# Parameter chains divided over VectorE and GpSimd, and both rotation products of a state-space block on GpSimd

## The chip, the cores and the metric

One core of a Trainium2 chip runs the whole program. The metric is device time in microseconds (us). Each time below is of one execution or is said to be a median.

## What is computed

The input `x` has the shape (16, 96, 16, 16): 16 batches, 96 channels, 256 tokens each. The output is `x + block(group_norm(x))`:

```python
fx = layernorm(tokens(group_norm(x)), ln1_g, ln1_b)          # groups of 3 channels, then over 96 channels
step = exp(log_step); lam_bar = exp(lam * step)               # 48 complex modes
mask = (step * abs(lam_im) / (2 pi) < 0.25)
B_bar = ((lam_bar - 1) / lam)[:, None] * Bc
x_t = lam_bar * x_(t-1) + B_bar fx_t                           # scan over the 256 tokens
y = 2 * real((Cc * mask) x_t) + D * fx
fy = layernorm(gelu(y) + fx, ln2_g, ln2_b)
z1, z2 = split(fy @ W_enc.T)
out = x + (z1 * gelu(z2)) @ W_dec.T + fy
```

## The kernel before

**Tiling.** The batches are two halves of eight, called H = 0 and H = 1. A half is 96 partitions by 2048 columns, in 4 tiles of 512. TensorE has four PSUM banks for each half. The scan takes the 256 tokens as 32 blocks of T = 8 tokens: inside a block VectorE runs seven steps (`scan`), across blocks four doublings follow (`doubled`, `doubling`).

**First stage of a half.** VectorE takes `bn_stats` of each batch (`statistics`). `group_norm(H)` makes mean, variance and 1/sigma of the groups, with two small matmuls on TensorE (`group_mean`, `group_variance`) and a Newton iteration on VectorE (`inverse_root`), in which each instruction waits for the one before it. `scale_centering(H, n)` then writes the matrix `pm` of batch n (96x96), and `center_batch(H, n)` multiplies the batch by it on TensorE. ScalarE evacuates the result twice (`squares`, `centered_values`). TensorE sums the squares (`variances`), VectorE makes 1/sigma of every token (`inverse_sigma`, twelve dependent instructions on 128x128), TensorE spreads it (`broadcast`), and VectorE multiplies (`scale_tile`, to `fx`). The matmuls of `inputs` multiply `fx` by the matrix `um`.

**The parameters.** `um` comes from a chain on 96x1 and 96x13 numbers. In `parameters()` VectorE makes exp(log_step), the angles (`ANG`, reduced to `RED`), the decays (`EXM`, `RK`); ScalarE makes two sines of `RED`; VectorE makes `COS` and `NSS` and the matrix `bst`. GpSimd makes `rotT` = identity times `COS` in one 96x768 product (L267), and VectorE adds swap times `NSS` in eight instructions (L789, recorded at L664). TensorE multiplies `bst` by `rotT` (L593, L594), and ScalarE evacuates `um` (L398, L400). `output_tables()` makes what the outputs need. When it has ended (`tables_ready`, L819), GpSimd makes the matrices `rotX` (three 96x576 instructions) and then `yl` (three 96x768 instructions, and a fourth for `yl[:, 1]`), L303 to L308.

**What sets the order.** The parameter chains are generators, and each of their steps is put by hand between instructions of the normalisation on VectorE (`parameter_steps`, L951 to L975): six steps first, one behind each `bn_stats`, one behind each instruction of `group_norm`, one after every second `scale_centering`, and the rest in `inverse_sigma(0, 0)`. All engines run their instructions in the order written. TensorE's order around the change (L561 to L611): warm-up matmuls, `group_mean(0)`, `group_variance(0)`, `center_batch(0, 0..5)`, `group_mean(1)` (which waits for the last `bn_stats` of the second half), `center_batch(0, 6..7)`, `group_variance(1)`, `variances(0, 0, ..)`, all eight `center_batch(1, n)`, two `variances` of the second half, the product for `um` (waits `bst_ready`, `rot_ready`), `broadcast(0, 0)`, `inputs(0, i)` with the other two `variances`, three small matmuls to `vecs`, then `direct` and `local_outputs` of three tiles (wait `yl_ready`), `seed_sum(0)` (waits `rotx_ready`) and `broadcast(0, 1)` (waits for `inverse_sigma(0, 1)`). Every TensorE instruction is recorded at line L424; an fp32 matmul shows as two records.

Of the kernel before, what the change touches and what calls it, by code (L numbers as in the profile page):

```python
# [34 lines left out]
ALU = mybir.AluOpType  # L35
# [7 lines left out]
T = 8  # L43
NA = L // T
HB = B // 2
# [10 lines left out]
WARM = (10, 2, 14)  # L56
WARM_N = 256
FIRST_PM = 4
GROUP = 3
NGRP = GROUP * L  # L60
GN_EPS = 1e-5
# [27 lines left out]
def s5_block(nc, x, small, mats, mask_in, out):  # L89
    ctx = ExitStack()  # L90
    with ctx:
# [22 lines left out]
        rotT = sb("rotT", [96, T, 96])  # L114
# [29 lines left out]
        par_steps = sem("par_steps")  # L144
# [5 lines left out]
        cos_ready = sem("cos_ready")  # L150
        rotcos_ready = sem("rotcos_ready")
# [4 lines left out]
        tables_ready = sem("tables_ready")  # L156
        rotx_ready = sem("rotx_ready")
        yl_ready = sem("yl_ready")
        dm_ready = sem("dm_ready")
        bcm_ready = sem("bcm_ready")  # L160
# [92 lines left out]
        def _(pool):  # L253
# [6 lines left out]
            def settle():  # L260
# [5 lines left out]
            pool.wait_ge(cos_ready, 1)  # L266
            nc.gpsimd.tensor_tensor(  # L267
                rotT[:, :, :], m(M_ID).unsqueeze(1).broadcast_to([96, T, 96]),
                tbl(COS, T).unsqueeze(2).broadcast_to([96, T, 96]), ALU.mult).then_inc(rotcos_ready, 1)
            pool.wait_ge(in_mats, 16)  # L270
# [45 lines left out]
        def _(act):  # L316
# [10 lines left out]
            nc.scalar.activation(tbl(SH), tbl(RED), ACT.Sin, scale=0.5).then_inc(sines_ready, 1)  # L327

# [46 lines left out]
            def gelu_y(H):  # L375

                for i in range(NT):
# [9 lines left out]

            group_bias(0)
# [7 lines left out]
            squares(1, 2, 6)  # L396
# [5 lines left out]
            squares(1, 6, HB)  # L402
# [19 lines left out]
        def _(pe):  # L422
# [26 lines left out]
            def center_batch(H, n):  # L449

                pe.wait_ge(pm_ready, HB * H + n + 1)
                mm(bank(H, n // 2)[0:96, L * (n % 2):L * (n % 2 + 1)], pm[:, HB * H + n, :],
                   xs[:, HB * H + n, :]).then_inc(centered[0], 1)
# [18 lines left out]
            def broadcast(k, H):  # L472

                pe.wait_ge(inv_ready[k], H + 1)
                for i in range(NT):
                    if k == 0:
                        pe.wait_ge(taken[0], HB * H + 2 * (i + 1))
                        if H == 0 and i >= 2:
                            pe.wait_ge(um_ready, i - 1)
# [110 lines left out]
            pe.wait_ge(taken[0], HB)  # L590
            pe.wait_ge(bst_ready, 1)
            pe.wait_ge(rot_ready, T)
            mm(bank(0, 2)[0:97, 0:480], bst[:, :], rotT[:, 0:5, :])  # L593
            mm(bank(0, 3)[0:97, 0:288], bst[:, :], rotT[:, 5:8, :]).then_inc(umat_done, 1)  # L594
            pe.wait_ge(bcm_ready, 1)
            broadcast(0, 0)
# [65 lines left out]
        def _(dve):  # L662
# [33 lines left out]
            norm, par = Steps(norm_steps), Steps(par_steps)  # L696

            def expm1(p, y, arg):

                par.next_ts(y, arg, 1 / 128, -80 / 128, ALU.mult, ALU.max)  # L700
                yield
                par.next_ts(p, y, 1 / 120, None, ALU.mult)
                yield
                for c in (1 / 24, 1 / 6, 1 / 2, 1.0):
                    par.next_stt(p, p, c, y, ALU.add, ALU.mult)
                    yield
                for _ in range(7):
                    par.next_stt(p, p, 2.0, p, ALU.add, ALU.mult)
                    yield

            def parameters():


                par.next_stt(scol(REC), s(LS), -1.0, s(LS), ALU.mult, ALU.max)
                yield
                yield from expm1(scol(EXP), scol(Y1), scol(REC))
                par.next_ts(scol(EXP1), scol(EXP), 1.0, None, ALU.add)
                par.add(scaled(scol(NEG), s(LS), 0.0, None, ALU.is_lt))
                par.add(scaled(scol(POS), s(LS), 0.0, None, ALU.is_ge))
                yield  # L720
                par.settle()
                par.add(nc.vector.reciprocal(scol(REC1), scol(EXP1)))
                yield
                par.next_tt(scol(T4), scol(REC1), scol(NEG), ALU.mult)
                yield
                par.next_stt(scol(STEP), scol(EXP1), scol(POS), scol(T4), ALU.mult, ALU.add)
                yield
                par.next_tt(scol(TH), s(LI), scol(STEP), ALU.mult)
                par.add(nc.vector.tensor_tensor(scol(RE), s(LR), scol(STEP), ALU.mult))
                yield  # L730
                par.next_ts(tbl(ANG), s(KV, NK), scol(TH), None, ALU.mult)
                par.add(scaled(tbl(XK), s(KV, NK), scol(RE), None, ALU.mult))
                yield

                par.next_ts(tbl(NRND), tbl(ANG), 1 / (2 * np.pi), ROUND, ALU.mult, ALU.add)
                yield
                par.next_ts(tbl(NRND), tbl(NRND), -ROUND, None, ALU.add)
                yield
                for part in (TWO_PI_HI, TWO_PI_MID, TWO_PI_LO):
                    par.next_stt(tbl(ANG), tbl(NRND), -float(part), tbl(ANG), ALU.mult, ALU.add)  # L740
                    yield
                par.settle()
                scaled(tbl(RED), tbl(ANG), PI_BELOW, -PI_BELOW, ALU.min, ALU.max).then_inc(angles_ready, 1)
                yield
                yield from expm1(tbl(EXM), tbl(TMP), tbl(XK))

                dve.wait_ge(sines_ready, 2)
                par.next_tt(tbl(SH2), tbl(SH), tbl(SH), ALU.mult)
                par.add(scaled(tbl(NSS), tbl(SIN), s(RHO), None, ALU.mult))
                par.add(scaled(tbl(RK), tbl(EXM), 1.0, None, ALU.add))  # L750
                yield
                par.next_ts(tbl(CM1), tbl(SH2), -2.0, None, ALU.mult)
                par.add(nc.vector.tensor_tensor(tbl(RSIN), tbl(RK), tbl(SIN), ALU.mult))
                par.add(nc.vector.tensor_tensor(scol(T2), s(LR), s(LR), ALU.mult))
                yield
                par.settle()
                scaled(tbl(COS), tbl(CM1), 1.0, None, ALU.add).then_inc(cos_ready, 1)
                par.add(nc.vector.tensor_tensor(scol(T3), tbl(RSIN, 1, 1), s(LI), ALU.mult))
                par.add(stt(scol(DEN), s(LI), s(LI), scol(T2), ALU.mult, ALU.add))
                yield  # L760

                dve.wait_ge(cos_ready, 1)
                par.next_tt(scol(T1), tbl(EXM, 1, 1), tbl(COS, 1, 1), ALU.mult)
                par.add(nc.vector.reciprocal(scol(DEN), scol(DEN)))
                yield
                par.next_tt(scol(T1), scol(T1), tbl(CM1, 1, 1), ALU.add)
                yield
                par.next_tt(scol(T4), scol(T1), s(LI), ALU.mult)
                par.add(stt(scol(CRE), scol(T1), s(LR), scol(T3), ALU.mult, ALU.add))
                yield  # L770
                par.next_stt(scol(CIM), tbl(RSIN, 1, 1), s(LR), scol(T4), ALU.mult, ALU.subtract)
                par.add(nc.vector.tensor_tensor(scol(CRE), scol(CRE), scol(DEN), ALU.mult))
                yield
                par.next_stt(scol(CIM), scol(CIM), scol(DEN), s(RHO), ALU.mult, ALU.mult)
                yield
                dve.wait_ge(in_mats, 16)
                par.next_ts(bt1[:, :], m(M_BS), scol(CIM), None, ALU.mult)
                yield
                par.next_stt(bst[:, 0:C], m(M_B), scol(CRE), bt1[:, :], ALU.mult, ALU.add)
                yield  # L780
                par.next_tt(bt1[:, :], bst[:, 0:C], m(M_B1), ALU.mult)
                yield
                par.settle()
                nc.vector.reduce_sum(bst[:, C:C + 1], bt1[:, :], axis=mybir.AxisListType.X).then_inc(bst_ready, 1)
                yield

                dve.wait_ge(rotcos_ready, 1)
                for b in range(T):
# [37 lines left out]
            def parameter_steps(count):  # L826

                for _ in range(count):
                    next(input_steps, None)
# [258 lines left out]
```

## Time and profile before

| what | us |
|---|---|
| median of 3 runs | 116.42 |
| the 3 runs | 110.52, 117.62, 116.42 |
| the profiled execution | 110.42 |
| its span, first to last instruction | 108.6 |
| TensorE, VectorE, ScalarE, GpSimd busy | 94.9, 77.6, 41.0, 31.9 |
| mean granted TensorE clock | 0.961 |

The profiled execution is 1.8 us longer than its span, and agrees with the shortest of the three runs. Times in the rows are counted from the start of the span. Engines are PE (TensorE), PEld (its weight loads), DVE (VectorE), ACT (ScalarE), POOL (GpSimd), SP (SyncE); a queue has a q behind its name.

### The profile page before, as it was taken

The numbers are of one execution on the slowest core, as the hardware profiler recorded it, in microseconds if no ns is written. First come the engines' busy times: TensorE is split into PE (matmuls) and PEld (weight loads), VectorE is DVE, ScalarE is ACT, GpSimd is POOL, SyncE is SP. The second block draws the span as 40 slices with busy tenths as digits, with TensorE's granted clock in tenths as the row PEclk, the third lists the DMA queues.
The fourth block names the chain that finished last, engine by engine and source line by source line (L and its number), as shares of the span: only waits on it lengthen the run. The fifth ranks groups of instructions, "written<-read, shape, count | busy, mean of one in ns | idle before, by whom it ended". The sixth has DMA issues, their size and how long they took to land.

```text
span 108.6 us, 1488 instructions
## 1 busy us (share of the span) xinstructions
PE 94.9 (87%) x502; PEld 56.2 (52%) x502; DVE 77.6 (71%) x260; ACT 41.0 (38%) x79; POOL 31.9 (29%) x26
## 2 busy tenths in 40 slices
PE   5999897269989929999899999999599999999960
PEld 4668766146555715676476655567324432533310
DVE  1688999999986899658677302389990289994590
ACT  2254167807449100024037009818049722024200
POOL 8600000400049992000018000007995000296000
PEclk9999999955799999999999999999999999999997
DMA  2997000000000000000000000000000000450135
GB/s 77 275 262 168 3 0 0 6 0 0 0 0 0 0 0 3 0 6 0 0 0 0 0 0 3 6 0 0 0 0 0 0 0 0 118 149 29 28 84 177
DMA packets 3767, 3.79 MB, mean 35 GB/s; under 512 B 496, under 2 KB 3664, under 8 KB 3760
## 3 DMA queue, kind: packets, MB, share of 16 engines
q1 hardware_dynamic: 3392, 3.49, 12.3%
q10 hardware_dynamic: 368, 0.20, 0.8%
q8 instruction: 4, 0.07, 0.3%
q14 instruction: 3, 0.02, 0.1%
HBM read 2.12 MB, written 1.57 MB: 34 GB/s over the span
## 4 chain that ended last, share of the span: by engine, by line
PE 70%; DVE 21%; issue 4%; ACT 1%; DVEq 1%
PE ps L424 70%; DVE st L836 2%; DVE fy L664 2%; DVE pm L885 2%; DVE sc L694 2%; DVE rs L664 1%; DVE upper L668 1%; DVE sq L664 1%; DVE tb L664 1%; DVE tb L668 1%; DVE y L982 1%; DVE gn L664 1%; DVE rs L694 1%; DVE fx L664 1%; DVE sc L664 1%
## 5 line engine op out<-in xcount | busy, mean ns | idle before, releaser
L424 PE MATMUL ps<-fy,mt 96*96 96x512 f32 x32 | 14.9, 600 | 1.3 <-DVE fy L664 1.3
L290 POOL TENSOR_TENSOR y<-gl,fx 96x512 f32<-96x512 f32 x4 | 6.1, 1524 | 29.8 <-ACT gl L379 29.8
L298 POOL TENSOR_TENSOR res<-fy,xs 96x512 f32<-96x512 f32 x8 | 10.7, 1359 | 11.6 <-DVE fy L664 11.5
L424 PE MATMUL ps<-xs,pm 96*96 96x256 f32 x32 | 10.8, 492 | 3.3 <-DVE pm L885 3.3
L385 ACT ACTIVATE y<-ps,vecs 96x512 f32<-96x512 f32 x8 | 5.5, 687 | 16.4 <-PE ps L424 16.4
L664 DVE SCALAR_TENSOR_TENSOR w<-ps,vecs,y 96x512 f32<-96x512 f32 x8 | 5.9, 743 | 7.4 <-ACT y L385 7.4
L424 PE MATMUL ps<-fx,dm 96*96 96x512 f32 x16 | 8.4, 605 | 2.6 <-issue 2.2
L933 DVE TENSOR_TENSOR Z<-Z,ps 96x240 f32<-96x240 f32 (+3 forms) x8 | 2.8, 355 | 9.5 <-PE ps L424 9.5
L424 PEld LDWEIGHTS ps<-fy,mt 96*96 96x96 f32 x32 | 5.0, 163 | 8.7 <-issue 6.8
L424 PEld LDWEIGHTS ps<-xs,pm 96*96 96x96 f32 x32 | 6.4, 214 | 5.9 <-DVE pm L885 3.8
L379 ACT ACTIVATE gl<-ps,db 96x512 f32<-96x512 f32 x8 | 5.5, 684 | 9.4 <-PE ps L424 9.4
L424 PE MATMUL ps<-wm 96*96 96x256 f32 x20 | 7.9, 586 | 1.2 <-DVE wm L949 1.2
L424 PE MATMUL ps<-fx,um 97*96 97x256 f32 x32 | 8.2, 390 | 0.2 <-DVE fx L664 0.2
L424 PE MATMUL ps<-w,yl 96*96 96x256 f32 x32 | 8.2, 379 | 0.0
L664 DVE SCALAR_TENSOR_TENSOR w<-w,tb,ps 96x256 f32<-96x256 f32 x14 | 6.6, 471 | 1.9 <-ACT w L366 1.2
L424 PE MATMUL ps<-w,mt 96*96 96x512 f32 x16 | 7.8, 602 | 0.0
L424 PEld LDWEIGHTS ps<-w,yl 96*96 96x96 f32 x32 | 5.2, 163 | 5.1 <-issue 4.0
L358 ACT ACTIVATE sq<-ps,vecs 96x512 f32<-96x512 f32 x8 | 5.5, 686 | 6.2 <-PE ps L424 6.2
L424 PE MATMUL ps<-y,mt 96*96 96x512 f32 x16 | 7.7, 595 | 0.1
L340 ACT ACTIVATE sq<-ps,gn 96x256 f32<-96x256 f32 x16 | 6.5, 470 | 2.7 <-PE ps L424 2.6
L424 PE MATMUL ps<-Z,yl 96*96 96x256 f32 x32 | 7.2, 379 | 0.0
L424 PEld LDWEIGHTS ps<-wm 96*96 96x96 f32 x20 | 5.1, 262 | 3.6 <-DVE wm L949 1.2
(112 smaller groups left out, 168.1 us busy)
## 6 DMA issues: line engine op xcount, KB each, us to landing
out_dram<-sq SPq DMA_DIRECT2D x8, 192.0 KB, 2.2
xs<-x_dram SPq DMA_DIRECT2D x3, 384.0 KB, 6.1
xs<-x_dram SPq DMA_DIRECT2D x2, 192.0 KB, 3.5
mt<-mats_dram SPq DMA_DIRECT2D x1, 338.6 KB, 6.8
mt<-mats_dram ACTq DMA_DIRECT2D x1, 180.0 KB, 3.9
sm<-small_dram ACTq DMA_DIRECT2D x1, 8.6 KB, 2.8
cmask<-mask_dram ACTq DMA_DIRECT2D x1, 9.0 KB, 4.9
```

What stands on the lines that cost most here:

```text
L290: nc.gpsimd.tensor_tensor(yv[:, RT * i:RT * (i + 1), :], cols(gl, H, i).rearrange("c (b m) -> c b m", b=RT), cols(fx, H, i).rearrange("c ( ...
L298: nc.gpsimd.tensor_tensor(cols(res, H, i), cols(fy, H, i), xs[:, HB * H + 2 * i:HB * H + 2 * i + 2, :].rearrange("c n l -> c (n l)"), ALU. ...
L340: nc.scalar.activation(t[:, H, :].rearrange("c (b n a) -> c n b a", b=T, n=HB)[:, n], bank(H, n // 2)[0:96, L * (n % 2):L * (n % 2 + 1)].r ...
L358: nc.scalar.activation(cols(sq, H, i), bank(H, i)[0:96, :], ACT.Square, bias=vecs[:, 2:3]).then_inc(squared[1], 1)
L379: nc.scalar.activation(cols(gl, H, i), bank(H, i)[0:96, :], ACT.Gelu, bias=db[:, 0:1]).then_inc(gl_ready, 1)
L385: nc.scalar.activation(cols(gz, H, i), bank(*Z2[H, i])[0:96, :], ACT.Gelu, bias=vecs[:, 1:2]).then_inc(gz_ready, 1)
L424: return nc.tensor.matmul(o, lhsT, rhs, start=start, stop=stop)
L664: return nc.vector.scalar_tensor_tensor(out=o, in0=a, scalar=sca, in1=b, op0=op0, op1=op1)
L668: return nc.vector.tensor_scalar(o, a, s1, None, op0)
L694: self.add(nc.vector.tensor_tensor(*a))
L836: nc.vector.bn_stats(st[:, HB * H + q, :], xs[:, HB * H + q, :]).then_inc(gn_stats, 1)
L933: nc.vector.tensor_tensor(zd, zd, o[:, :, d:], ALU.add).then_inc(z_ready, 1)
```

## The change

The work of `parameters()` and `output_tables()` is divided.

- VectorE keeps one generator `step_chain()`: step size, angle unit `TH` (`angle_unit_ready`), decays (`decay_ready`), and the chain to `bst`. It is taken two steps behind each of the first eight `bn_stats`, then one at a time.
- GpSimd makes the angles (ten dependent 96x13 instructions), `COS` and `NSS` (`cos_ready`), `rotS` = swap times `NSS` and `rotC` = identity times `COS` (two 96x768 products), the output tables, `db` and `dm`; after `inv_ready[0]` it makes `yl` first and `rotX` second. The eight VectorE instructions on `rotT` are gone.
- ScalarE makes `pm` of batches 2 to 7 of the first half (FIRST_PM = 2).
- TensorE adds 14 warm-up matmuls ahead of `center_batch(1, 0)`, does four `center_batch(1, n)`, then the product for `um` from `rotS` and `rotC` with twice the matmuls, then `broadcast(0, 0)` with `center_batch(1, 4)` and `(1, 5)` inside, then the last two and two `variances`.

```diff
-WARM = (10, 2, 14)
+WARM = (10, 2, 14, 14)
-FIRST_PM = 4
+FIRST_PM = 2
...
# GpSimd
-            pool.wait_ge(cos_ready, 1)
+            pool.wait_ge(angle_unit_ready, 1)
+            ts(tbl(ANG), s(KV, NK), scol(TH), None, ALU.mult)
+            settle()
+            ts(tbl(NRND), tbl(ANG), 1 / (2 * np.pi), ROUND, ALU.mult, ALU.add)
+            settle()
+            ts(tbl(NRND), tbl(NRND), -ROUND, None, ALU.add)
+            for part in (TWO_PI_HI, TWO_PI_MID, TWO_PI_LO):
+                settle()
+                ts(tbl(RED), tbl(NRND), -float(part), None, ALU.mult)
+                settle()
+                tt(tbl(ANG), tbl(RED), tbl(ANG), ALU.add)
+            settle()
+            nc.gpsimd.tensor_scalar(tbl(RED), tbl(ANG), PI_BELOW, -PI_BELOW, ALU.min,
+                                    ALU.max).then_inc(angles_ready, 1)
...
+            pool.wait_ge(sines_ready, 2)
+            tt(tbl(SH2), tbl(SH), tbl(SH), ALU.mult)
+            settle()
+            ts(tbl(CM1), tbl(SH2), -2.0, None, ALU.mult)
+            settle()
+            nc.gpsimd.tensor_scalar(tbl(COS), tbl(CM1), 1.0, None, ALU.add).then_inc(cos_ready, 1)
+            nc.gpsimd.tensor_scalar(tbl(NSS), tbl(SIN), s(RHO), None, ALU.mult).then_inc(cos_ready, 1)
...
+                rotS[:, :, :], m(M_SW).unsqueeze(1).broadcast_to([96, T, 96]),
+                tbl(NSS, T).unsqueeze(2).broadcast_to([96, T, 96]), ALU.mult).then_inc(rot_ready, 1)
...
+                rotC[:, :, :], m(M_ID).unsqueeze(1).broadcast_to([96, T, 96]),
+                tbl(COS, T).unsqueeze(2).broadcast_to([96, T, 96]), ALU.mult).then_inc(rot_ready, 1)
...
+            pool.wait_ge(inv_ready[0], 1)
...
-            pool.wait_ge(tables_ready, 1)
+            combine(yl, M_C, tbl(CU, T), M_CS, tbl(SU, T), T).then_inc(yl_ready, 1)
             combine(rotX, M_ID, tbl(XCO, NX), M_SW, tbl(XSI, NX), NX).then_inc(rotx_ready, 1)
-            combine(yl, M_C, tbl(CU, T), M_CS, tbl(SU, T), T).then_inc(yl_ready, 1)
# ScalarE, behind the two sines
+            for n in range(FIRST_PM, HB):
+                scale_centering(n)
...
-            squares(1, 2, 6)
+            squares(1, 2, 4)
             act.wait_ge(umat_done, 1)
...
# TensorE
+            warm_up(WARM[3], bank(1, 0))
             center_batch(1, 0)
             group_bias(1)
-            center_batch(1, 1)
-            for i in range(1, NT):
-                if i == NT - 1:
-                    pe.wait_ge(bias_ready, 2)
-                center_batch(1, 2 * i)
-                center_batch(1, 2 * i + 1)
+            for n in range(1, 4):
+                center_batch(1, n)
+            pe.wait_ge(taken[0], HB)
+            pe.wait_ge(bst_ready, 1)
+            pe.wait_ge(rot_ready, 2)
+            for part, first, last in ((2, 0, 5), (3, 5, 8)):
+                o = bank(0, part)[0:97, 0:96 * (last - first)]
+                mm(o, bst[:, :], rotS[:, first:last, :], stop=False)
+                last_mm = mm(o, bst[:, :], rotC[:, first:last, :], start=False)
+            last_mm.then_inc(umat_done, 1)
+            pe.wait_ge(bcm_ready, 1)
+            broadcast(0, 0, lambda: (center_batch(1, 4), center_batch(1, 5)))
+            pe.wait_ge(bias_ready, 2)
+            center_batch(1, 6)
+            center_batch(1, 7)
             variances(0, 1, 0)
             variances(0, 1, 1)
# VectorE
+            step_chain_on(6)
             for q in range(HB):
                 statistics(0, q)
-                parameter_steps(1)
+                step_chain_on(2)
             dve.wait_ge(in_early, 16)
             statistics(1, 0)
+            group_norm(0, lambda j: step_chain_on(1), lambda: (statistics(1, 1), statistics(1, 2)))
+            for n in range(FIRST_PM):
                 scale_centering(0, n)
+            for q in range(3, HB):
                 statistics(1, q)
+                step_chain_on(1)
+            group_norm(1, lambda j: step_chain_on(1), lambda: step_chain_on(2))
+            scale_centering(1, 0)
+            scale_centering(1, 1)
+            inverse_sigma(0, 0, lambda j: scale_centering(1, j + 3) if j < 1 else step_chain_on(1))
+            for n in range(4, HB):
+                scale_centering(1, n)
```

## Rows read from the trace of the kernel before

**Rows 1.** The page's first part: busy us, share of the span, instructions.
```profile
PE 94.9 (87%) x502; PEld 56.2 (52%) x502; DVE 77.6 (71%) x260; ACT 41.0 (38%) x79; POOL 31.9 (29%) x26
```

**Rows 2.** The chain that ended last: start us, us, what.
```profile
22.35 0.27 DVE pm L885
...
22.66 8.81 PE ps L424 x38
...
32.21 5.63 PE ps L424 x46
37.84 2.21 issue
40.05 6.44 PE ps L424 x26
```

**Rows 3.** Windows: stretch, length, busy us of the engines, granted clock, DMA.
```profile
21.50:22.00 0.50, 0.00 (x0) 0.00 (x0) 0.47 (x5) 0.00 (x0) 0.00 (x0) 0.74 0.00 0
...
22.60:28.00 5.40, 5.34 (x14) 3.76 (x15) 5.36 (x29) 2.56 (x7) 0.00 (x0) 0.50 0.00 0
...
28.50:29.00 0.50, 0.50 (x3) 0.33 (x2) 0.50 (x3) 0.50 (x2) 0.00 (x0) 0.93 0.00 0
```

**Rows 4.** Timeline of GpSimd and of VectorE beside it: start us, us, instruction.
```profile
4.30 0.12 POOL L264 MEMSET Z<- 96x16 f32 x1
...
18.85 1.47 POOL L267 TENSOR_TENSOR rotT<-mt,tb 96x768 f32<-96x768 f32 x1 [14.42 <-DVE tb L668]
...
19.07 1.27 DVE L694 TENSOR_TENSOR sc<-tb 96x1 f32<-96x1 f32 x1
...
31.47 1.15 POOL L280 TENSOR_TENSOR rotX<-mt,tb 96x576 f32<-96x576 f32 x1 [11.15 <-DVE db L819]
...
31.72 2.72 DVE L664 SCALAR_TENSOR_TENSOR fx<-xc,sm,ps 96x512 f32<-96x512 f32 x4 [0.22 <-PE ps L424]
...
38.15 1.80 POOL L283 TENSOR_TENSOR yl<-yl 96x768 f32<-96x768 f32 x1
...
38.47 1.63 DVE L664 SCALAR_TENSOR_TENSOR rs<-rs 128x128 f32<-128x128 f32 x1
```

**Rows 5.** Timeline of VectorE in the first stage.
```profile
3.57 0.15 DVE L664 SCALAR_TENSOR_TENSOR sc<-sm 96x1 f32<-96x1 f32 x1 [2.43 <-DMA sm<-small_dram]
3.76 0.15 DVE L669 TENSOR_SCALAR sc<-sc 96x1 f32<-96x1 f32 x1
...
7.83 0.14 DVE L664 SCALAR_TENSOR_TENSOR sc<-sc 96x1 f32<-96x1 f32 x1
7.89 0.41 DVE L836 BATCH_NORM_STATS2 st<-xs 96x6 f32<-96x256 f32 x1
...
9.28 0.17 DVE L864 TENSOR_REDUCE gn<-ps 96x8 f32<-96x16 f32 x1 [0.50 <-PE ps L424]
...
17.48 0.17 DVE L864 TENSOR_REDUCE gn<-ps 96x8 f32<-96x16 f32 x1 [0.15 <-PE ps L424]
```

**Rows 6.** Timeline of TensorE, first and second half's first stage.
```profile
14.20 1.95 PE L424 MATMUL ps<-xs,pm 96*96 96x256 f32 x8
...
18.62 1.10 PE L424 MATMUL ps<-sq,mt 96*32 96x128 f32 x32
22.66 1.17 PE L424 MATMUL ps<-xs,pm 96*96 96x256 f32 x2 [2.94 <-DVE pm L885]
...
29.93 1.53 PE L424 MATMUL ps<-rotT,bst 96*97 96x480 f32 x4
31.29 0.61 PE L424 MATMUL ps<-parts,bcm 128*96 128x128 bf16 x8
...
34.58 2.83 PE L424 MATMUL ps<-fx,um 97*96 97x256 f32 x12
```

**Rows 7.** Groups of VectorE by shape, first 32 us: busy us, mean ns.
```profile
L664 DVE SCALAR_TENSOR_TENSOR rotT<-mt,tb,rotT 96x96 f32<-96x96 f32 x8 | 2.5, 309 | 0.0
```

**Rows 8.** Timeline of VectorE in two calls of inverse_sigma: end of one, a bare one.
```profile
28.76 0.34 DVE L664 SCALAR_TENSOR_TENSOR parts<-upper,cmask,rs 128x128 bf16<-128x128 bf16 x1
...
70.15 0.29 DVE L669 TENSOR_SCALAR rs<-ps 128x128 f32<-128x128 f32 x1 [0.76 <-PE ps L424]
...
75.03 0.35 DVE L664 SCALAR_TENSOR_TENSOR parts<-upper,cmask,rs 128x128 bf16<-128x128 bf16 x1
```

More of the change, by code:

```diff
@@ L113, in s5_block @@
         mt = sb("mt", [96, NM])
-        rotT = sb("rotT", [96, T, 96])
+        rotC = sb("rotC", [96, T, 96])
+        rotS = sb("rotS", [96, T, 96])
         rotX = sb("rotX", [96, 2, NX, 96])
@@ L159, in s5_block @@
         dm_ready = sem("dm_ready")
+        db_ready = sem("db_ready")
+        angle_unit_ready = sem("angle_unit_ready")
+        cos_ready = sem("cos_ready")
+        decay_ready = sem("decay_ready")
+        pm_act = sem("pm_act")
         bcm_ready = sem("bcm_ready")
@@ new lines, in _ @@
+            tt(scol(MR), scol(MASK), s(NRHO), ALU.mult)
+            ts(scol(MI), scol(MASK), -1.0, None, ALU.mult)
+            ts(tbl(SSG), tbl(SIN), s(NRHO), None, ALU.mult)
+            settle()
+            ts(tbl(CU), tbl(COS), scol(MR), None, ALU.mult)
+            ts(tbl(SU), tbl(SIN), scol(MI), None, ALU.mult)
+            pool.wait_ge(decay_ready, 1)
+            for dst, unit in ((XCO, COS), (XSI, SSG)):
+                ts(tbl(dst, 1, 0), tbl(unit, 1, T), tbl(RK, 1, 1), tbl(RK, 1, 0), ALU.mult, ALU.mult)
+                ts(tbl(dst, 1, 1), tbl(unit, 1, K16), tbl(RK, 1, 1), tbl(RK, 1, T), ALU.mult, ALU.mult)
+                tt(tbl(dst, 4, 2), tbl(unit, 4, K16), tbl(RK, 4, K16), ALU.mult)
@@ L375, in gelu_y @@
             def gelu_y(H):
+                act.wait_ge(db_ready, 1)
                 for i in range(NT):
@@ L401, in _ @@
                                  ACT.Copy).then_inc(um_ready, 1)
-            squares(1, 6, HB)
+            squares(1, 4, HB)
             centered_values(1, 2, HB)
@@ L470, in variances, with broadcast @@
                     last.then_inc(variance[k], 1)
-            def broadcast(k, H):
+            def broadcast(k, H, between=None):
                 pe.wait_ge(inv_ready[k], H + 1)
@@ L477, in broadcast @@
                         pe.wait_ge(taken[0], HB * H + 2 * (i + 1))
+                        if H == 0 and i == 2:
+                            between()
                         if H == 0 and i >= 2:
@@ L694, in next_tt @@
                     self.add(nc.vector.tensor_tensor(*a))
[L696 to L788, printed above, removed]
-                    stt(rotT[:, b, :], m(M_SW), tbl(NSS, 1, b), rotT[:, b, :],
-                        ALU.mult, ALU.add).then_inc(rot_ready, 1)
-                    yield
@@ L824, in _ @@
-            input_steps, output_steps = parameters(), output_tables()
-            def parameter_steps(count):
-                for _ in range(count):
-                    next(input_steps, None)
+            norm = Steps(norm_steps)
             def statistics(H, q):
@@ L855, in inverse_root, with group_norm @@
                 norm.next_stt(y, u, 5.0, y, ALU.add, ALU.mult)
-            def group_norm(H, between=lambda: None, after=lambda: None):
+            def group_norm(H, between=lambda j: None, after=lambda: None):
                 var, t, u, minus, scale, shift = [gn[:, H, k, 0:HB] for k in
@@ L949, in _, with step_chain_on @@
+            steps = step_chain()
+            def step_chain_on(count):
+                for _ in range(count):
+                    next(steps, None)
             nc.vector.memset(wm[:, :], 1.0).then_inc(wm_ready, 1)
             dve.wait_ge(in_small, 16)
-            parameter_steps(6)
+            step_chain_on(6)
             for q in range(HB):
                 statistics(0, q)
-                parameter_steps(1)
+                step_chain_on(2)
             dve.wait_ge(in_early, 16)
             statistics(1, 0)
-            group_norm(0, lambda: parameter_steps(1), lambda: (statistics(1, 1), parameter_steps(2)))
@@ L967, in _ @@
-            for n in range(FIRST_PM):
-                scale_centering(1, n)
-                parameter_steps(1)
-            inverse_sigma(0, 0, lambda j: scale_centering(1, FIRST_PM + 1 + j) if j < HB - FIRST_PM - 1
-                          else parameter_steps(1))
-            for _ in input_steps:
-                pass
-            for _ in output_steps:
+                step_chain_on(1)
+            group_norm(1, lambda j: step_chain_on(1), lambda: step_chain_on(2))
+            scale_centering(1, 0)
@@ L975, in _ @@
+            scale_centering(1, 1)
+            inverse_sigma(0, 0, lambda j: scale_centering(1, j + 3) if j < 1 else step_chain_on(1))
+            for n in range(4, HB):
+                scale_centering(1, n)
+            for _ in steps:
                 pass
```

162 lines of the change are left out of this document (108 added, 54 removed).

## The prediction, made before the change was run

> **What bounds the kernel now.** I read the page's busy shares first, then the chain that ended last, then windows and timelines of the stretch that the diff touches. TensorE is busy for 94.9 of 108.6 us [rows 1], so it has some 14 us without work, and only what fills those, or what TensorE does slowly, can be won. The chain shows where in this stretch: TensorE starts on the second half at 22.66, when VectorE has written the first `pm` at 22.35 [rows 2]. I call this start of the first `pm` of the second half X; before, X = 22.35. From there TensorE is on the chain almost alone, up to a hole of 2.21 us at 37.84 which the chain calls "issue" [rows 2]. The hole ends at 40.05, just as GpSimd's sum to `yl` ends (38.15 + 1.80 = 39.95) [rows 4]: it is the wait `yl_ready`. The GpSimd chain to it began only at 31.47 [rows 4], and does `rotX` first. Ahead of X TensorE stood idle for 2.94 us [rows 6], and the granted clock fell from 2.4 to 1.2 GHz in that idle time (0.74 in 21.5 to 22.0, 0.50 from 22.6 to 28) and came back near 28.5 (0.93 there) [rows 3]. So the eight `center_batch` of the second half ran at half clock. That cost little, since the product for `um` waited for VectorE's eight rotation instructions in any case: it began at 29.93 = X + 7.6 [rows 6].
>
> **The change part by part.** The sum is made in two pieces: what moves X, and what stands between X and `broadcast(0, 1)`. All behind that is unchanged in code.
>
> *VectorE up to the first group_norm.* Two chain steps per `bn_stats` in place of one. A dependent step costs 3.76 - 3.57 = 0.19 [rows 5]; a step behind a `bn_stats` starts 0.06 ahead of the next one (7.83, 7.89) [rows 5]. Eight extra steps of 0.19 are 1.5 us; four second instructions in the first steps (0.07 each, an estimate: half of the 0.14 that one lasts, since independent ones overlap) make 0.3 more. Of it, 0.45 fell before into a wait for the load of batch 4, and the rest into time that VectorE waited for TensorE ahead of 9.28 [rows 5], 0.5 us. That leaves about 1.0: group_norm(0) starts near 10.35. It has fewer multi-instruction steps in it, which gives back 0.2. First `pm`: +0.8.
>
> *First half's pm on ScalarE and the statistics.* VectorE saves six `pm` and four steps and goes to the remaining five `bn_stats` at about 14.0. Without any disturbance these end at 16.1. TensorE gets there later: six batches at 0.49 (1.95 for four) [rows 6] from 13.95 and one small matmul end at 16.9, and `group_mean(1)` is behind them. Before, the reduction behind it was at 17.48 [rows 5]. ScalarE's six `pm` cost it about 1.3 us ahead of the first squares; it has slack there.
>
> *GpSimd's small chain.* No 96x13 GpSimd operation is in the trace. From below it is bounded by the memset of 96x16, 0.12; from above by a whole 96x576 product, 1.15; a line through 1.15 for 576 columns and 1.47 for 768 gives 0.21 for 13 columns [rows 4], and I take this, with 0.08 between dependent ones: 0.29 a step. The angle unit is there at about 9.2, ten steps end at 12.1, the sines at 12.8, cosines at 14.0, and the two rotation products run from 14.0 to 17.0 (1.47 each) [rows 4]. At 0.12 a step all is 1 us earlier; at 1.15 it would be over 10 us later.
>
> *What the products block.* While GpSimd ran `rotT`, a 96x1 VectorE product that otherwise takes 0.15 took 1.27, and ended as GpSimd did; beside the `yl` sum a 128x128 instruction took 1.63 in place of 0.29. Beside `rotX`, VectorE's four instructions with one input in PSUM went on at 0.7 each [rows 4]. So here a VectorE instruction that has all its inputs in SBUF waits for a GpSimd product to end. In the new kernel both products lie beside the last five `bn_stats`, and between these stands a chain step each. The step behind the first waits to 15.5, the next to 17.0, the last three go free: the statistics end near 18.3 in place of 16.1, the reduction at 18.6. group_norm(1), before 17.48 to 22.35, lost 1.1 to such a block and carried more steps; I take 3.7. X = 18.6 + 3.7 = 22.3: **as before**. Bounds: 21.0 (TensorE's 16.9 + 0.4 + 3.7, no block) to 25.6 (third rival).
>
> The Trainium skill, page "SBUF — State Buffer", section "Who interferes with whom", says that an instruction of VectorE with two SBUF inputs, or one in a 2-port mode, and a GpSimd one that reads SBUF lock each other out, whoever starts first, while one with at most one SBUF input (`bn_stats` is one) goes on. The rows agree as to products. It speaks against moving small work to GpSimd beside a busy VectorE: each of some 25 small operations may then hold up VectorE, or be held up by it. By that rule X would be the later side of my range; if only the two large products count, it is 22.3.
>
> *From X on, TensorE's own work.* Eight batches 3.9, bias 0.25, `um` product twice 1.53 less overlap = 2.8, broadcast 1.3 (two of 0.61), `variances` of four tiles 1.4 (a little over 1.10), `inputs` 3.8 (2.83 for three tiles), `vecs` 0.5 [rows 6]: 14.0 us, all at full clock. It starts at X + 0.3 and ends at X + 14.3. Before, this point was 37.84 = X + 15.5, and the hole made it X + 17.7 [rows 2]. Is TensorE kept waiting? The `um` product starts at X + 2.6, long after rotS, rotC (17.0) and `bst` (inside group_norm(1)). The eight rotation instructions (2.5 us busy) [rows 7] and four of the eight `pm` no longer stand in or ahead of `inverse_sigma(0, 0)`: a bare one lasts 70.15 to 75.38 with one block of 1.0 in it, 4.2 net; it ends at X + 4.7, before at 29.1 = X + 6.75 [rows 8]. TensorE gets to `broadcast(0, 0)` at X + 5.4: no wait. `pm` 4 to 7 are written just as GpSimd begins with `yl`, and may be blocked for one product, 1.47: 0.4 of wait on `center_batch(1, 5)`. ScalarE is through with the second half's evacuations at X + 12.2 and gives the scan its start at X + 12.6 (before X + 12.8).
>
> *yl.* GpSimd starts at X + 4.75, `yl` is there after 1.47 + 1.47 + 1.80 at X + 9.6: the hole is gone. What is late next is `inverse_sigma(0, 1)` with the scans: from X + 14.1, 5.5 us (before 8.85, of it 3.3 in three blocks beside `yl`), with 0.6 for a block beside `yl[:, 1]`: X + 20.2. TensorE comes there at X + 14.7 + 5.2 + 0.8 = X + 20.7; before it was X + 23.7. `rotX` (X + 13.4) is in time.
>
> *Sum.* 17.7 - 14.3 - 0.4 = 3.0 us won, X unmoved: 110.4 - 3.0 = **107.4**. That is against the profiled execution of 110.42, which is like the 110.52 of the three runs; their median, 116.42, stands 6 us over it, and the trace doesn't say by what. Two of three runs lie there. A second loss of clock in the hole at 37.84 would be one candidate, which the change would take away, but that is a guess, and the range has to reach runs of that kind.
>
> **The rivals.**
> *The clock falls again.* For: TensorE is idle from 16.9 to 18.2 too, and then has only the end of the first half and the warm-up, 1.3 us, up to X. Against: it fell some 2 us into an idle stretch [rows 3], and the warm-up halves the longest one. If TensorE has 6.8 us at 1.2 GHz from X on as before, its 14.0 us of work become 17.4, and this time nothing hides it: X + 17.7 + 0.4, the point of before. 110.4 + 0.3 = **110.7**.
> *The win is given back at the scans.* If blocks beside `yl`, `rotX` and `yl[:, 1]` hit the scans' neighbours as often as before (three times, 3.3 us), the second broadcast comes at X + 22.4 and 1.3 is left: **109.1**. Against: GpSimd is nearly done by then.
> *The small chain on GpSimd is late: slower.* Place: VectorE's step `T1` waits for `cos_ready`, and behind it stand two `bn_stats`; ScalarE waits for the angles ahead of the first half's `pm`. It decides from about 0.5 us a step on, by operation cost or by VectorE and GpSimd holding each other up. At 0.6 the cosines come at 18.0, the reduction at 19.3, the products at 18 to 21 fall into group_norm(1) and block it twice for 1.3: X = 19.3 + 3.7 + 2.6 = 25.6, 3.3 late, with an idle time that costs the clock, 3.4: 110.4 - 3.0 + 3.3 + 3.4 = **114.1**. Nothing in the trace has this size of operation, so I can't exclude it.
> *The products let VectorE by.* If the statistics are not held up, X = 21.0: **106.1**.
>
> **How the numbers follow.** Forecast 107.4: 0.45. Clock: 0.17. Scans: 0.12. Late chain: 0.16. Let by: 0.10. A difference of about 2% is what a measurement of this kernel can tell from none, here 2.2 us. Faster by over 2%: the forecast and "let by" nearly whole, half of the scans, and a share from runs of the longer kind going: 0.64. Within 2%: 0.21. Slower: 0.15. The forecast's own range is 105.8 to 109.0; the clock and part of the late chain, and runs of the longer kind, take the range to 114.5 above; 105.5 below.
>
> **What would show it.** Right: no hole ahead of `fx,dm` matmuls; `yl` done some 8 us earlier; VectorE instructions of 1.3 us beside rotS and rotC, between `bn_stats`; X near 22.3; full clock from 18 to 40; broadcast(0, 1) near 43. Wrong: GpSimd steps over 0.5 us apart; ScalarE's `pm` waiting for the sines past 14; half clock behind the warm-up; a new wait ahead of broadcast(0, 1).

## The result, and the profile after

| | kernel before | changed kernel |
|---|---|---|
| runs, us | 110.52, 110.80, 116.42, 117.62 | 116.20, 116.99, 117.11, 117.38 |
| median | 113.61 | 117.05 |
| profiled execution, its span | 110.42, 108.6 | 117.11, 114.9 |
| granted clock of the profiled execution | 0.961 | 0.911 |

The change made the kernel slower: ratio 1.057, 95% interval 1.047 to 1.066. The forecast was 107.4. Because the granted TensorE clock differs between executions of one and the same kernel (the kernel before ran with 0.86 to 0.965) and the time goes with it, each ratio and its interval compare only the fast executions of both kernels, here 110.52 and 110.80 with all four of the changed one, while each median is over all executions. Profiles are of one execution each, and are compared at marked points.

The chain that ended last in the changed kernel, start us, us, what:

```profile
12.88 0.18 DVE tb L738
...
13.08 0.18 DVE gn L743
...
13.29 0.18 DVE tb L738
...
13.49 0.18 DVE gn L743
...
14.75 1.48 DVE gn L738
16.25 1.41 DVE tb L738
...
19.50 33.20 PE ps L488 x206
...
53.52 5.23 PE ps L488 x24
```

Two things are to be seen. The hole of 2.21 us of [rows 2] is gone: TensorE is on the chain without a break for 33 us. But this begins at 19.50 already with the *first* half, whose first `pm` was there at 12.8 before. In group_norm(0), lines `gn` (the normalisation) and `tb` (the parameter chain) alternate every 0.2 us, each waiting for the other, and two of them last 1.48 and 1.41 us.

GpSimd and VectorE side by side, timeline of the changed kernel:

```profile
9.79 0.35 POOL L273 TENSOR_SCALAR tb<-sm,sc 96x13 f32<-96x13 f32 x1 [4.17 <-DVE sc L920]
10.23 0.21 POOL L275 TENSOR_SCALAR tb<-tb 96x13 f32<-96x13 f32 x1
...
14.73 1.47 POOL L308 TENSOR_TENSOR rotS<-mt,tb 96x768 f32<-96x768 f32 x1
16.16 1.47 POOL L311 TENSOR_TENSOR rotC<-mt,tb 96x768 f32<-96x768 f32 x1
...
13.90 0.16 DVE L738 SCALAR_TENSOR_TENSOR gn<-gn 96x8 f32<-96x8 f32 x1
14.09 0.21 DVE L738 SCALAR_TENSOR_TENSOR tb<-tb 96x13 f32<-96x13 f32 x1
14.34 0.17 DVE L768 TENSOR_TENSOR gn<-gn 96x8 f32<-96x8 f32 x1
...
14.75 1.47 DVE L738 SCALAR_TENSOR_TENSOR gn<-gn 96x8 f32<-96x8 f32 x1
16.25 1.40 DVE L738 SCALAR_TENSOR_TENSOR tb<-tb 96x13 f32<-96x13 f32 x1
```

GpSimd's products start at 14.73, where the forecast put them (14.0, with a chain start 0.6 earlier). They were to find VectorE behind group_norm(0), among the `bn_stats`; they found it in the middle of group_norm(0), and stopped it twice.

TensorE in the changed kernel, and its clock by windows:

```profile
10.50 0.47 PE L488 MATMUL ps<-st,mt 96*96 96x16 f32 x2 [2.04 <-DVE st L777]
...
19.50 1.22 PE L488 MATMUL ps<-xs,pm 96*96 96x256 f32 x4 [2.33 <-DVE pm L826]
...
20.75 3.71 PE L488 MATMUL ps<-xs,pm 96*96 96x256 f32 x8
24.25 0.40 PE L488 MATMUL ps<-st,mt 96*96 96x16 f32 x2
...
28.79 4.80 PE L488 MATMUL ps<-mt 96*96 96x96 f32 x28
33.38 0.91 PE L488 MATMUL ps<-xs,pm 96*96 96x256 f32 x2
...
46.25 1.08 PE L488 MATMUL ps<-fx,dm 96*96 96x512 f32 x2
...
52.30 1.06 PE L488 MATMUL ps<-parts,bcm 128*96 128x128 bf16 x16
```
```profile
10.00:17.00 7.00, 6.30 (x38) 6.22 (x38) 6.44 (x24) 0.79 (x3) 5.89 (x18) 0.51 0.03 8
17.00:20.00 3.00, 0.67 (x4) 0.41 (x4) 2.73 (x14) 0.70 (x3) 1.90 (x6) 1.00 0.00 0
20.00:34.00 14.00, 14.00 (x85) 11.43 (x84) 9.47 (x49) 7.33 (x21) 1.63 (x6) 0.51 0.00 1
34.00:52.00 18.00, 18.00 (x117) 11.79 (x116) 12.34 (x29) 7.60 (x21) 9.83 (x7) 1.00 0.00 1
```

The third column from the end is the granted clock (DMA share and GB/s follow). With each of the two idle stretches (2.04 and 2.33 us, in brackets) goes a stretch at 1.2 GHz: the first begins near 10.2, inside the idle time, and lasts 7 us, the second begins near 20.4, when TensorE is back at work, and lasts 14 us. In the second lie four batches in 3.71 us, which took 1.95 at 2.4 GHz [rows 6]; and the added warm-up, which starts at 28.79 and takes 4.80 us. VectorE started the first `pm` of the second half at 29.55; TensorE came to it at 33.38. So the added warm-up stands on the path itself.

Marked points, us from the start of the span (the last column is the changed kernel with one edit undone, e1 below):

| start of | before | changed | e1 |
|---|---|---|---|
| group_norm(0) | 9.28 | 11.01 | 10.78 |
| first pm, first half | 12.83 | 19.19 | 14.06 |
| first pm, second half (X) | 22.35 | 29.55 | 22.74 |
| center_batch(1, 0) | 22.66 | 33.38 | 23.87 |
| broadcast(0, 1) | 46.09 | 52.30 | 42.71 |
| span | 108.6 | 114.9 | 105.3 |

The part from center_batch(1, 0) to broadcast(0, 1) fell from 23.4 to 18.9: that half of the change won 4.5 us. The part ahead of it lost 10.7: the first `pm` of the first half came 6.4 later, the way from there to X took 0.8 more, and TensorE came to the second half 3.8 behind X and not 0.3 (3.5 more).

### The profile page after: what moved, and what is told of

Same layout as the page of the kernel before. It is cut to its first block, busy times and chain, and to the rows that moved or that the text cites. A ratio compares the mean times of both kernels' runs of the same rounds, so it can differ in the third digit from the quotient of the medians.

```text
span 114.9 us, 1549 instructions
## 1 busy us (share of the span) xinstructions
PE 103.5 (90%) x534; PEld 64.7 (56%) x534; DVE 76.5 (67%) x219; ACT 42.4 (37%) x85; POOL 41.4 (36%) x56
## 3 DMA queue, kind: packets, MB, share of 16 engines
HBM read 2.12 MB, written 1.57 MB: 32 GB/s over the span
## 4 chain that ended last, share of the span: by engine, by line
PE 69%; DVE 18%; DMA 5%; issue 2%; SPq 1%; DVEq 1%; ACT 1%
PE ps L488 69%; DMA xs<-x_dram 5%; DVE tb L738 3%; DVE st L777 2%; DVE gn L738 2%; DVE fy L738 2%; DVE rs L738 1%; DVE upper L742 1%; DVE sq L738 1%; DVE y L1001 1%; DVE rs L768 1%; SPq L246 1%; DVE fx L738 1%; ACT y L447 1%; DVEq L91 1%
## 5 line engine op out<-in xcount | busy, mean ns | idle before, releaser
L346 POOL TENSOR_TENSOR y<-gl,fx 96x512 f32<-96x512 f32 x4 | 6.6, 1661 | 32.6 <-ACT gl L441 32.6
L354 POOL TENSOR_TENSOR res<-fy,xs 96x512 f32<-96x512 f32 x8 | 10.7, 1360 | 11.6 <-DVE fy L738 11.5
L488 PE MATMUL ps<-xs,pm 96*96 96x256 f32 x32 | 11.4, 501 | 2.3 <-DVE pm L826 2.3
L488 PE MATMUL ps<-mt 96*96 96x96 f32 x60 | 10.4, 371 | 0.0
L488 PEld LDWEIGHTS ps<-mt 96*96 96x96 f32 x60 | 9.9, 279 | 0.4 <-issue 0.4
L488 PE MATMUL ps<-wm 96*96 96x256 f32 x20 | 7.3, 545 | 1.2 <-DVE wm L974 1.2
L1001 DVE TENSOR_TENSOR y<-gl,fx 96x512 f32<-96x512 f32 x4 | 6.8, 1728 | 1.7 <-ACT gl L441 1.7
```

The source lines that it names most:

```text
L346: nc.gpsimd.tensor_tensor(yv[:, RT * i:RT * (i + 1), :], cols(gl, H, i).rearrange("c (b m) -> c b m", b=RT), cols(fx, H, i).rearrange("c ( ...
L354: nc.gpsimd.tensor_tensor(cols(res, H, i), cols(fy, H, i), xs[:, HB * H + 2 * i:HB * H + 2 * i + 2, :].rearrange("c n l -> c (n l)"), ALU. ...
L488: return nc.tensor.matmul(o, lhsT, rhs, start=start, stop=stop)
L1001: nc.vector.tensor_tensor(yv[:, RT * i:RT * (i + 1), :], cols(gl, H, i).rearrange("c (b m) -> c b m", b=RT), cols(fx, H, i).rearrange("c ( ...
```

## The experiments

My theory after seeing this had four parts. The change had also replaced the two semaphores `norm_steps` and `par_steps` by one, `norm_steps`, which the diff shown ahead of the prediction leaves out: `settle()` waits for all that was counted, so each instruction of group_norm now waits for the chain step put between, and the two chains, which overlapped, became one. This puts GpSimd's products inside group_norm(0); both together leave TensorE idle and its clock falls; the warm-up then runs at half clock. Rivals: only the clock costs; or GpSimd's small instructions hold VectorE up.

**e1: a counter of its own for the chain.**
```diff
+        par_steps = sem("par_steps")
...
-            norm = Steps(norm_steps)
+            norm, par = Steps(norm_steps), Steps(par_steps)
...
-                norm.next_stt(scol(REC), s(LS), -1.0, s(LS), ALU.mult, ALU.max)
+                par.next_stt(scol(REC), s(LS), -1.0, s(LS), ALU.mult, ALU.max)
# and so on through step_chain
```


> The changed kernel with the chain steps counted on a semaphore of their own again, as before the change. Theory (four parts: shared counter, rotation products inside group_norm(0), half clock behind an idle stretch, warm-up at half clock): group_norm(0) loses the wait on the other chain, 11 pairs from 0.41 back to about 0.20 us a pair, so the first pm comes about 2 us earlier (19.2 to 17.2) and the time falls by 1.5 to 2.5 us to about 115. Rival (only the clock costs): the chain is shorter but the batches at half clock stay the bound, time 116.5 to 117.5. Rival (small GpSimd operations hold VectorE up): the pairs stay at 0.4 us.

Measured: median 109.22 (107.42 to 109.97), against 111.81 of the kernel before; ratio 0.973, interval 0.952 to 0.994. About 8 us came back, four times what I had expected: with the first `pm` at 14.06 the products no longer fell into group_norm(0), and the clock, down from 12.3, was back at 2.4 GHz from 15.7 on, so that the second warm-up took 2.62 us. Timeline of VectorE and GpSimd in e1:

```profile
12.53 0.16 DVE L739 SCALAR_TENSOR_TENSOR gn<-gn 96x8 f32<-96x8 f32 x1
12.63 0.17 DVE L739 SCALAR_TENSOR_TENSOR tb<-tb 96x13 f32<-96x13 f32 x1
12.73 0.16 DVE L769 TENSOR_TENSOR gn<-gn 96x8 f32<-96x8 f32 x1
...
14.41 0.42 DVE L778 BATCH_NORM_STATS2 st<-xs 96x6 f32<-96x256 f32 x1
14.75 1.44 DVE L743 TENSOR_SCALAR tb<-tb 96x13 f32<-96x13 f32 x1
16.10 0.41 DVE L778 BATCH_NORM_STATS2 st<-xs 96x6 f32<-96x256 f32 x1
16.44 1.17 DVE L941 TENSOR_TENSOR tb<-tb 96x13 f32<-96x13 f32 x1
...
14.69 1.47 POOL L309 TENSOR_TENSOR rotS<-mt,tb 96x768 f32<-96x768 f32 x1
```

A pair takes 0.20 again (12.53 to 12.73), while ten small GpSimd instructions run beside it: these hold nothing up, and that rival falls. The products now lie between the `bn_stats` and stop one chain step each, as the prediction had it. The profiled execution took 107.42 (forecast 107.4), the shortest of the four.

**e2: 15 warm-ups at the start; e3: none ahead of the second half.** The rest as in the changed kernel.
```diff
-WARM = (10, 2, 14, 14)
+WARM = (15, 2, 14, 14)    # e2
+WARM = (10, 2, 14, 0)     # e3
```


> The changed kernel with 15 instead of 10 warm-up matmuls at the start, so that TensorE is not idle for 2 us ahead of group_mean(0). Theory (four parts): the first fall of the clock near 10 us goes, but the warm-up behind group_variance(0) then ends sooner and leaves over 4 us of idle time ahead of the first pm, so the clock falls there at about 16 to 17 us; time 116 to 118. Rival (only the clock costs): one fall fewer, time about 112 to 114.

> The changed kernel without the 14 warm-up matmuls ahead of center_batch(1, 0). Theory (four parts): the first batch of the second half starts near 29.7 instead of 33.4, when its pm is there, but at half clock, which then lasts some 4 us longer into the batches and the um product; of the 3.7 us about 1.5 to 2.5 are won: time 114.5 to 115.5. Rival (the warm-up pays for itself by the clock): 117 or more.

Measured: e2 117.40 (ratio 1.056, 1.040 to 1.071), e3 116.94 (1.054, 1.040 to 1.067). e2 is what the theory said: the first fall is gone, TensorE then waits 4.56 us for the first `pm`, and the clock is down from 16.3 to 33.3. In e3 I was wrong. The second half starts at 30.43, three us sooner, but the clock stays down to 38.5, and the product for `um` runs at half speed (1.81 in place of 0.97 for 480 columns). The warm-up does buy the clock back; with the clock down it costs about what it gives. Neither of these two edits of the warm-up gave time back while the counter was shared.

**e4: products behind group_norm(0).**
```diff
             pool.wait_ge(cos_ready, 2)
+            pool.wait_ge(gn_shift, 1)
```


> The changed kernel with the two rotation products waiting for gn_shift of the first half, so that they lie beside the second half's statistics and not inside group_norm(0). Theory (four parts): the two VectorE instructions of 1.4 us in group_norm(0) go, first pm near 16.6 instead of 19.2; the products then stop chain steps between the last bn_stats, 2 to 3 us, which TensorE partly hides at half clock; time 115 to 116.5. Rival (only the clock costs): unchanged, 116.5 to 117.5.

Measured: 113.86, from 111.31 to 118.48, too spread for a verdict. The profile divides the loss. From the first reduction to the first `pm` group_norm(0) takes 8.2 us in the changed kernel (11.01 to 19.19), 5.5 in e4 (10.72 to 16.22), 3.3 in e1 (10.78 to 14.06) and 3.55 before. So the products inside it cost 2.7 and the shared counter by itself 2.2. With the clock back at 22.2 in this execution, the warm-up takes 2.62 us, not 4.80.

**e5: the kernel before, with one counter.** The converse of e1.
```diff
-            norm, par = Steps(norm_steps), Steps(par_steps)
+            norm = par = Steps(norm_steps)
```


> The kernel before with nothing changed but that its two chains count on one semaphore, as in the changed kernel. Theory (a shared counter makes two interleaved chains one): the pairs in group_norm(0) go from 0.20 to 0.41 us, first pm near 14.9 instead of 12.8; group_norm(1) and inverse_sigma(0, 0), where eight rotation instructions stand between the steps, are stretched too, some 1.5 to 2 us each; time up by 4 to 6 us. Rival (the counter matters only together with the GpSimd products inside group_norm(0)): up by 0 to 1.5 us, since TensorE waits in that stretch anyway.

Measured: 117.80 (115.23 to 118.67) against 112.41 (110.95 to 113.45): 5.4 us slower by the medians, with no other edit. TensorE in e5:

```profile
16.29 2.02 PE L424 MATMUL ps<-xs,pm 96*96 96x256 f32 x4 [0.95 <-DVE pm L885]
...
28.92 1.17 PE L424 MATMUL ps<-xs,pm 96*96 96x256 f32 x2 [2.47 <-DVE pm L885]
...
37.32 2.88 PE L424 MATMUL ps<-rotT,bst 96*97 96x480 f32 x4
```

The first `pm` starts at 15.98, 5.65 behind the reduction at 10.33; before it was 3.55. In the profile of e6 below, the kernel before with two counters, it is 3.55 again. The clock stays at half from 12.9 to 43.6, so the 5.4 us are the longer chains and the clock together, and no run takes the two apart. The counter costs this much without GpSimd's products in group_norm(0), and that rival falls too.

**e6: the kernel before, yl ahead of rotX.**
```diff
-            combine(rotX, M_ID, tbl(XCO, NX), M_SW, tbl(XSI, NX), NX).then_inc(rotx_ready, 1)
             combine(yl, M_C, tbl(CU, T), M_CS, tbl(SU, T), T).then_inc(yl_ready, 1)
+            combine(rotX, M_ID, tbl(XCO, NX), M_SW, tbl(XSI, NX), NX).then_inc(rotx_ready, 1)
```


> The kernel before with yl made ahead of rotX on GpSimd and nothing else. Theory (the hole of 2.2 us ahead of the first fx,dm matmuls is the wait yl_ready): the hole goes, yl is there at 36.3 instead of 40, time down by 1 to 2.2 us; rotX, now ready near 40.1, is still in time for seed_sum near 43. Rival (inverse_sigma(0, 1), stopped three times by GpSimd products, takes the wait's place): time within 0.7 us of before, with a new wait ahead of broadcast(0, 1).

Measured: 109.91 against 112.41, ratio 0.979, interval 0.968 to 0.991. The hole went, as the theory said, and the rival's wait came in its place in part:

```profile
37.87 0.59 PE L424 MATMUL ps<-sm,mt 96*96 96x1 f32 x6
38.32 1.08 PE L424 MATMUL ps<-fx,dm 96*96 96x512 f32 x2
...
45.52 1.09 PE L424 MATMUL ps<-parts,bcm 128*96 128x128 bf16 x16 [1.00 <-DVE parts L664]
```

The hole ahead of `fx,dm` is gone, and 1.00 of it is back as a wait for `inverse_sigma(0, 1)`, in which four instructions beside GpSimd's products still take 0.60 to 1.16 us in place of 0.2 to 0.3. From center_batch(1, 0) to broadcast(0, 1) it is 22.2 us in place of 23.4.

**e7: e1 with 15 warm-ups at the start; e8 and e11: e1 without those ahead of the second half.** The diffs are those of e2 and e3, on e1.

> The changed kernel with chain steps on their own counter and 15 warm-up matmuls at the start. Theory: with the first pm at 14.1 there is no idle stretch long enough any more, TensorE stays at full clock throughout; TensorE then waits for the second half's statistics near 17 to 18.8, since these are stopped by the two products; against the kernel with its own counter alone 0 to 0.7 us are won, time 107 to 108.5. Rival (the clock falls in the wait at 17 to 19): slower than that kernel, 109 to 112.

> The changed kernel with chain steps on their own counter and without the 14 warm-up matmuls ahead of center_batch(1, 0). Theory: in this state the warm-up costs 1.1 us (TensorE starts the second half at 23.87, its pm is there at 23.0) and holds the clock over an idle stretch of 1.5 us that alone would not bring it down: time 0.5 to 1.1 us under the kernel with its own counter, 107 to 108.5. Rival (the warm-up is what holds the clock): the clock falls near 23 and the time is 110 to 113.

> Own counter and no warm-up ahead of the second half once more, in more rounds, to set its time against the kernel before: theory 106.7 to 107.5, ratio 0.95 to 0.97; if the first result was luck of the clock, 108.5 to 110.

Measured: e7 112.01 (109.74 to 113.96) where e1 had 109.22 (107.42 to 109.97). In its profile the clock fell at 19.8, during the first half's last work, after a wait of 1.20 us for the statistics, and the second warm-up took 4.80 us. The rival was right. e8 107.05 (ratio 0.957, 0.945 to 0.969); but the same kernel in more rounds, e11, 111.02 (107.60 at a clock of 0.978, 110.57 to 111.32 at 0.937, 112.69 at 0.906, 114.70 at 0.894). In e11's profile TensorE waited 1.25 us up to 23.70 and the clock fell again at 24.2; in e8's it waited 1.57 us up to 22.47 and the clock held. So the median of e8 was luck of the clock. Whether the warm-up is worth having is not shown: with it the ten executions of e1 and e13 have a median of 108.6, without it the ten of e8 and e11 one of 110.2, but these ran on three different chips (7; 10 and 12).

**e9, e10, e12: the last five bn_stats one behind another** (on e1), so that no chain step, which a product can stop, stands between them. The three `WARM` lines are of three different kernels.
```diff
             for q in range(3, HB):
                 statistics(1, q)
-                step_chain_on(1)
-WARM = (10, 2, 14, 14)
+WARM = (10, 2, 14, 0)     # e9
+WARM = (15, 2, 14, 0)     # e10
+WARM = (15, 2, 14, 8)     # e12
```


> As the kernel with its own counter and no warm-up ahead of the second half, and the five last bn_stats one behind another, their chain steps moved into group_norm(1). Theory: the statistics then end near 16 instead of 18.6, as no instruction that needs the port of GpSimd's products stands between them; TensorE gets there at 18.2 at half clock, so only 0.0 to 0.4 us are won, and the five more steps in group_norm(1) cost as much: same time within 0.7 us, 106.5 to 107.7. Rival (VectorE's block beside the products sets the time): 1.5 to 2.5 us less, 104.5 to 105.5.

> The kernel of the run before (own counter, statistics one behind another, no warm-up ahead of the second half) with 15 warm-up matmuls at the start. Theory: TensorE is at full clock up to group_mean(1), gets there near 17 and finds the statistics done, so the first pm of the second half comes near 21 and no idle stretch ahead of it is over 2 us: time 105 to 106.5. Rival (the clock falls in the idle stretch ahead of the second half, as in the run with 15 warm-ups): 109 to 112.

> Own counter, the last five bn_stats one behind another, 15 warm-ups at the start and 8 ahead of the second half. Theory: the 8 lie in the 1.7 us in which TensorE waits for the first pm of the second half, so they cost nothing at full clock and leave 1.0 us idle; where the clock holds the time is 105.5 to 106.7, and it holds in more runs than without them (median 106 to 108). Rival (they run at half clock as often as not and push the second half back): median 109 or more.

Measured: e9 110.84 (107.25 to 115.17), inconclusive. e10 107.43 (106.60 to 114.95), ratio 0.967 (0.954 to 0.979); e12 107.86 (106.46 to 115.97), ratio 0.964 (0.953 to 0.975). Both theories had promised a little more (105 to 106.5, and 105.5 to 106.7 where the clock holds). In e10 the mechanism is plain, with GpSimd's two products below VectorE:

```profile
14.04 1.72 DVE L778 BATCH_NORM_STATS2 st<-xs 96x6 f32<-96x256 f32 x5
17.13 0.17 DVE L806 TENSOR_REDUCE gn<-ps 96x8 f32<-96x16 f32 x1 [1.37 <-PE ps L489]
...
14.39 1.47 POOL L309 TENSOR_TENSOR rotS<-mt,tb 96x768 f32<-96x768 f32 x1
15.82 1.47 POOL L312 TENSOR_TENSOR rotC<-mt,tb 96x768 f32<-96x768 f32 x1
```

Five `bn_stats` take 1.72 us, up to 15.76, with the first product running beside all but the first 0.35 of it: they are not stopped, where in e1 they and the steps among them took from 14.41 to 18.8. (The second product starts when they have ended.) The Trainium skill, page "SBUF — State Buffer", section "Who interferes with whom", has this as a rule: only VectorE instructions with two SBUF inputs, or in a 2-port mode, contend with a GpSimd instruction that reads SBUF. The trace agrees for `bn_stats`, and for the `tensor_tensor` that was stopped in e1 (1.17 us) and for the `tensor_scalar` (1.44 us); that the latter ran in a 2-port mode, no run shows.

**e13 and e14: e1 and the changed kernel again, on one chip.**

> The changed kernel with its own counter for the chain, nothing else, again beside the changed kernel on the same chip. Theory: the counter alone is worth 6 to 9 us of median against the changed kernel and leaves a time 1 to 4% under the kernel before. If the first result was luck of the clock: under 4 us against the changed kernel.

> The changed kernel as it is, on the chip of the two others. Theory: 116 to 118 us again, with a granted clock of 0.91 to 0.93 in its runs, since its idle stretches ahead of group_mean(0) and of the first pm (2.0 and 2.3 us) bring the clock down in every execution.

Measured: e13 108.50, ratio 0.968 (0.956 to 0.980), one of its six runs at 118.34 with a clock of 0.882; e14 116.89 (116.29 to 121.29), ratio 1.048 (1.038 to 1.058). The counter alone, with all that follows from it, is worth 8.4 us of median in the changed kernel. The run at 118.34 is a warning: it was the profiled one, its span is 116.1 where e1's is 105.3, its first `pm` is at 14.26, as in e1 (14.06), and yet TensorE is at half clock from 11.6 to 38.9. So the clock alone can cost this kernel as much as the whole measured difference. The other five executions of e13 took 106.98 to 108.84, all six of e14 at least 116.29, and therefore the difference of the medians is no such luck.

Of the versions run, e10, e12 and e13 (107.4, 107.9, 108.5) all beat both kernels by median, and their intervals don't set them apart. None of them holds in every execution: e12 ran at full clock throughout once (107.05), and at 0.925 twice (115.28, 115.97). The profile of the one at 115.28 shows more than the clock:

```profile
14.39 2.97 DVE L827 TENSOR_SCALAR pm<-mt,gn 96x96 f32<-96x96 f32 x2
...
14.39 1.46 POOL L309 TENSOR_TENSOR rotS<-mt,tb 96x768 f32<-96x768 f32 x1
15.82 1.47 POOL L312 TENSOR_TENSOR rotC<-mt,tb 96x768 f32<-96x768 f32 x1
```

Here VectorE waited 0.46 for group_mean(0), which came behind the last of the 15 warm-ups; group_norm(0) began at 11.10 and not at 10.40 as in e10, and the two `pm`, which take 0.46 there, start just as the products do: both are stopped. TensorE waits 1.44 and 0.76 us for them, and the clock is down from 17.6 to 34.7. The execution at 115.97 has no profile, but the same clock. What stays untested is this version with the products waiting until the two `pm` are written.

## Why the prediction was wrong

- **The step that failed** is "It has fewer multi-instruction steps in it, which gives back 0.2. First `pm`: +0.8." It carried the cadence of the trace of before, 0.2 us for a pair of instructions, over to code in which both chains count on one semaphore. The full diff showed it (`norm, par` became `norm`, each `par.next_...` became `norm.next_...`), and I read it as a rename. group_norm(0) took 8.2 us where I had 3.3: 2.2 by the counter (e1 against e4), 2.7 by the products that it thus met (the changed kernel against e4). First `pm` +6.4, not +0.8.
- **Products among the statistics.** They started as long behind the angle unit as I had said (4.9 us, forecast 4.8), at 14.73; the failed step put group_norm(0) under them. With it mended (e1) they stop two chain steps for 2.3 us, the statistics end at 18.8 against 18.3 foreseen, X is 22.74 against 22.3. One sentence was too wide: that a VectorE instruction with all its inputs in SBUF waits for the product doesn't hold for `bn_stats`, which the sum had rightly let run.
- **The start of group_norm(0)**: 11.01 against 10.35. In that execution the load of batch 4 landed 1.1 us later (7.80 for 6.69), and VectorE still waited 0.56 for it, a wait that I had taken to be gone; that is most of the miss. In e1 it is 10.78.
- **Small GpSimd instructions**: 0.20 to 0.35 each, 0.29 to 0.35 from start to start where dependent, 0.44 for the first; I took 0.29. Nearly right, and the "late chain" rival fell: it needed over 0.5.
- **The clock rival** had the mechanism, but I gave it one stretch of 6.8 us and 0.17 (and its own terms, X + 18.1 against X + 17.7, give 110.8 and not 110.7). In the changed kernel two stretches of 7 and 14 us stood, and a cost I had put at nothing: the added warm-up at half clock, 4.80 us, so that TensorE came 3.8 us behind the start of the first `pm`. I had set the warm-up down as something that only shortens the idle time.
- **From X on** the prediction was right in kind and low in size: 20.4 us forecast from center_batch(1, 0) to broadcast(0, 1), 18.9 measured. The mis-sized term is the sum of 14.0 us of TensorE work, which measured 12.9 (33.38 to 46.25): I added durations of groups whose ends overlap the next. The other 0.4 is the wait on `center_batch(1, 5)`, which didn't come, as TensorE was 3.8 behind X; where it was close behind, the wait was 0.69 (e8) and 0.30 (e4). The hole was the wait `yl_ready` (e6), and nothing took its place here.
- **The total.** 107.4 was meant for a kernel with two counters. That kernel (e1 and e13) had medians of 109.2 and 108.5, and three of its ten executions took 107.42 or less. That the profiled one hit 107.42 is in part luck: X came 0.4 later than forecast and TensorE came to it 0.8 later, by the warm-up, while the stretch behind was 1.6 shorter; broadcast(0, 1) at 42.71 against 43.0 is what these leave.

## What to carry to other kernels

A semaphore that counts is an order: two chains on one counter are one chain, at 0.41 us a pair instead of 0.20 here, and a diff that folds two counters into one has to be costed like an added wait on every instruction between. Before placing warm-up matmuls, ask what they cost at half clock (4.80 us for 2.62 here) and what is ready behind them. Where GpSimd runs long products beside VectorE, put `bn_stats` or instructions with an input in PSUM there, and keep `tensor_scalar` and `tensor_tensor` on SBUF out of that stretch, if need be by a wait on GpSimd (untested here): where only the timing kept them apart, they met in an execution of e12. And look at the granted clock of an execution before explaining its time.

## What the runs showed of the hardware that I had not expected

- The clock can fall after TensorE has gone back to work: in e10 it waited 1.72 us up to 21.54 and the clock fell near 22.9; in the changed kernel the wait ended at 19.50 and the clock fell near 20.4. One and the same kernel waited 1.25 us up to 23.70 and then lost the clock (e11), and waited 1.57 us up to 22.47 and kept it (e8).
- Beside ten small GpSimd instructions VectorE's dense chain of small ones kept its 0.20 us a pair (e1), though all of them have their inputs in SBUF. A `tensor_scalar` with one 96x96 input was stopped by a product (e12: 2.97 us for two that take 0.46 in e10).
- One kernel's median over several rounds moved by 4 us between two sessions on two chips (107.05 and 111.02), with its clock at 0.98 in most executions of the one and at 0.94 or less in most of the other.
